# Moving the mask and the slot values of a graph kernel's setup from VectorE to GpSimd

## The reference

```
x = layernorm(x + L0(x))   # gated graph network: 4 steps of  a[dst] += W[type] @ h[src] + b[type];  h = GRU(a, h)
x = layernorm(x + L1(x))   # GIN, two convolutions: h + sum over edges, then a two-layer perceptron
x = layernorm(x + L2(x))   # GCN: symmetric normalization, relu, batch norm
x = layernorm(x + L3(x))   # SAGE: weighted mean of the neighbours
```

## Time and profile before

| | us |
|---|---|
| median of 3 runs | 9466.73 (9453.7 to 9488.25) |
| profiled execution, its own time | 9465.41 |
| its span, first to last instruction | 9463.6 |
| TensorE busy | 6959.9 (74%) |
| VectorE busy | 5864.7 (62%) |
| GpSimd busy | 4695.3 (50%) |
| ScalarE busy | 4484.3 (47%) |

### The profile page before, as it was taken

The page is one execution under the profiler, slowest core; times in us unless marked ns, Lnnn a source line. Parts: engine busy times, 40 slices in busy tenths (PEclk is TensorE's granted clock), DMA queues, the critical chain, the costliest instruction groups (busy, mean ns, idle before and its releaser), DMA issues.

```text
span 9463.6 us, 174694 instructions
## 1 busy us (share of the span) xinstructions
PE 6959.9 (74%) x57107; PEld 5494.3 (58%) x57108; DVE 5864.7 (62%) x15303; ACT 4484.3 (47%) x11415; POOL 4695.3 (50%) x4469
## 2 busy tenths in 40 slices
PE   4666666668877887887777777666688876648988
PEld 2333333347767776776666566545466655537887
DVE  7888888856666665665777433222245533347998
ACT  0000000036655655565888666555566655534443
POOL 0000000027756765665666566567666656655554
PEclk7887777779999998998999888787778878879999
DMA  3211111159999999999999999999999999959897
GB/s 86 66 46 46 51 46 46 46 169 269 265 257 264 272 263 260 267 267 256 253 258 252 260 274 278 261 277 274 271 267 264 270 254 269 272 151 230 224 224 192
DMA packets 1185494, 2014.92 MB, mean 213 GB/s; under 512 B 421508, under 2 KB 864807, under 8 KB 1181690
## 3 DMA queue, kind: packets, MB, share of 16 engines
q1 hardware_dynamic: 916698, 1097.24, 46.9%
q10 hardware_dynamic: 126656, 689.26, 20.0%
q0 software_dynamic: 141280, 217.70, 10.3%
HBM read 1232.72 MB, written 770.89 MB: 212 GB/s over the span
## 4 chain that ended last, share of the span: by engine, by line
DMA 32%; issue 24%; PE 17%; DVE 14%; ACT 8%; DVEq 4%; SPq 2%; POOL 0%; ACTq 0%; POOLq 0%
DMA bounce<-work 17%; DMA work<-bounce 14%; PE ps_pair L1024 5%; ACT work L1270 5%; PE ps_agg L1041 3%; DVE hs L1779 2%; PE ps_agg L1038 2%; DVE work L1788 2%; DVE agg_sb L1820 2%; ACT L1296 1%; DVEq L1795 1%; DVEq L1777 1%; PE ps_gate L1101 1%; DVE work L1802 1%; ACT gate L1296 1%
## 5 line engine op out<-in xcount | busy, mean ns | idle before, releaser
L846 POOL DMA_INDIRECT work<-node_rows,work x4410 | 4638.7, 1052 | 2686.9 <-issue 1464.8
L1270 ACT ACTIVATE work<-ps_pair 120x384 bf16<-120x384 f32 x7344 | 3364.2, 488 | 1671.5 <-PE ps_pair L1024 1047.0
L1024 PE MATMUL ps_pair<-rows_now,work 128*128 128x192 bf16 x14688 | 2614.2, 267 | 727.4 <-ACT work L1270 435.4
L1024 PEld LDWEIGHTS ps_pair<-rows_now,work 128*128 128x128 fp8e4 x14688 | 1288.4, 104 | 1201.9 <-issue 1056.5
L1041 PE MATMUL ps_agg<-work 120*128 120x192 bf16 x6272 | 967.2, 287 | 394.7 <-DMA work<-bounce 381.2
L1769 DVE TENSOR_TENSOR work<-iota_bf,dl_all 120x2048 bf16<-120x2048 bf16 x882 | 1075.2, 1219 | 30.4 <-DMA rows_now<-node_rows 16.6
L1038 PE MATMUL ps_agg<-work 120*128 120x192 bf16 (+1 forms) x6272 | 843.0, 259 | 223.4 <-DMA work<-bounce 209.2
L852 POOL MEMSET work<- 128x32 bf16 x2 | 0.2, 124 | 1955.8 <-SPq L677 1955.8
L1041 PEld LDWEIGHTS ps_agg<-work 120*128 120x128 bf16 x6272 | 660.1, 115 | 464.7 <-issue 359.6
L1058 PE MATMUL ps_agg<-work 128*128 128x192 bf16 (+1 forms) x7840 | 911.9, 247 | 0.7 <-issue 0.6
L1038 PEld LDWEIGHTS ps_agg<-work 120*128 120x128 bf16 x6272 | 579.5, 102 | 250.5 <-issue 165.0
(11 more groups left out here) (314 smaller groups left out, 10909.0 us busy)
## 6 DMA issues: line engine op xcount, KB each, us to landing
bounce<-work ACTq DMA_DIRECT2D x918, 727.5 KB
work<-bounce SPq DMA_DIRECT2D x882, 727.5 KB
work<-src_onehots SPq DMA_DIRECT2D x918, 256.0 KB
work<-node_rows,work POOLq DMA_INDIRECT x4410
work<-grid_vals SPq DMA_DIRECT2D x49, 960.0 KB, 5.0
node_rows<-stage SPq DMA_DIRECT2D x686, 48.0 KB
rows_now<-node_rows SPq DMA_DIRECT2D x42, 768.0 KB, 13.6
src_onehots<-work SPq DMA_DIRECT2D x17, 1536.0 KB, 8.4
```

The costliest lines, as they stand in the source:

```text
L846: pool.indirect_dma_start(out=ring[:, at.slot3() * LB + b, 0:3 * H], out_offset=None, in_=table_of(at.p), in_offset=bass.IndirectOffsetOnA ...
L1024: last = mm(bank[:, a * 3 * H:(a + 1) * 3 * H], oh[s.buf()][:, 2 * m + a, :], rows_now[:, s.chunk() * CHUNK + 2 * m + a, :], start=a == 0, ...
L1270: a_(raw[s.raw()][0:ROWS, m // 2, 2 * (m % 2):2 * (m % 2) + 2, 0:3 * H], ps_pair[m % 2][0:ROWS, 0:6 * H].rearrange("p (b f) -> p b f", b=2 ...
```

## The change

In the loop over pairs:

- The comparison of columns (L1592) moves ahead of the first rank product. The mask (L1595) goes to GpSimd (`slot_values`), between the new semaphores `same_made` and `ahead_made`. The reduction into `ahead` (L1597) moves behind the second rank product, and waits for the mask.
- The source one-hots are made in two parts, for the first tile of the pair between the two rank products, for the second tile where both were.
- The values of the slots (L1632) and of the rest (L1661) are made by GpSimd, two instructions each. The place one-hots have a buffer each (`grid_at`, `left_at`). TensorE waits for the lane one-hots (`lanes_made`) and for the values of the rest (`left_made`) by two semaphores. SyncE's wait for `left_made` now is a wait for GpSimd.
- GpSimd does this for the pairs in order, ahead of its wait for the end of the setup.

```diff
@@ GpSimd, new
+        def slot_values(q, par):
+
+            two = win[par]
+            pool.wait_ge(same_made, q + 1)
+            pool.sem_inc(pool_ran, 1)
+            g.tensor_tensor(same, same, earlier.to_broadcast([P, 2, WC, WC]), ALU.mult).then_inc(ahead_made, 1)
+            pool.wait_ge(grid_known, q + 1)
+            pool.sem_inc(pool_ran, 1)
+            for t in range(2):
+                last = g.tensor_tensor(grid_now[:, t, :, :, :],
+                                       grid_at[:, t, :, :].rearrange("p n (o u) -> p n o u", o=1)
+                                       .to_broadcast([P, WC, GV, SLOTS]),
+                                       two[t][:, :, DL:W2 + 1].rearrange("p n (v o) -> p n v o", o=1)
+                                       .to_broadcast([P, WC, GV, SLOTS]), ALU.mult)
+            last.then_inc(grid_made, 1)
+            pool.wait_ge(left_known, q + 1)
+            pool.sem_inc(pool_ran, 1)
+            for t in range(2):
+                last = g.tensor_tensor(left_now[:, t, :, :, :],
+                                       left_at[:, t, :, :].rearrange("p n (b o) -> p n b o", o=1)
+                                       .to_broadcast([P, WC, LB, LV]),
+                                       two[t][:, :, 0:LV].rearrange("p n (o v) -> p n o v", o=1)
+                                       .to_broadcast([P, WC, LB, LV]), ALU.mult)
+            last.then_inc(left_made, 1)
...
@@ TensorE, place_pair
                 last.then_inc(grid_placed[t], 1)
+            pe.wait_ge(lanes_made, q + 1)
             pe.wait_ge(left_made, q + 1)
             if not first:
@@ VectorE, rank_pair
+            v.tensor_tensor(same, key.rearrange("p t (n o) -> p t n o", o=1).to_broadcast([P, 2, WC, WC]),
+                            key.rearrange("p t (o n) -> p t o n", o=1).to_broadcast([P, 2, WC, WC]), ALU.is_equal
+                            ).then_inc(same_made, 1)
             rank_in_lower(0)
-            v.tensor_tensor(same, key.rearrange("p t (n o) -> p t n o", o=1).to_broadcast([P, 2, WC, WC]),
-                            key.rearrange("p t (o n) -> p t o n", o=1).to_broadcast([P, 2, WC, WC]), ALU.is_equal)
-            dve.drain()
-            v.tensor_tensor(same, same, earlier.to_broadcast([P, 2, WC, WC]), ALU.mult)
-            dve.drain()
-            v.tensor_reduce(out=ahead, in_=same, axis=AX.X, op=ALU.add)
+            if spare_work is not None:
+                spare_work(0)
             dve.wait_ge(rank_folded[0], q + 1)
             rank_in_lower(1)
+            dve.wait_ge(ahead_made, q + 1)
+            dve.sem_inc(dve_ran, 1)
+            v.tensor_reduce(out=ahead, in_=same, axis=AX.X, op=ALU.add)
             if spare_work is not None:
-                spare_work()
+                spare_work(1)
...
-            at_place(rank)
-            dve.drain()
-            for t in range(2):
-                last = v.tensor_tensor(grid_now[:, t, :, :, :],
-                                       places[:, t, :, :].rearrange("p n (o u) -> p n o u", o=1)
-                                       .to_broadcast([P, WC, GV, SLOTS]),
-                                       two[t][:, :, DL:W2 + 1].rearrange("p n (v o) -> p n v o", o=1)
-                                       .to_broadcast([P, WC, GV, SLOTS]), ALU.mult)
-            last.then_inc(grid_made, 1)
+            at_place(grid_at, rank).then_inc(grid_known, 1)
...
-            at_place(batch)
+            at_place(left_at, batch).then_inc(left_known, 1)
             dve.drain()
             for t in range(2):
-                one_hots(lane_hot[t], P, lane_i, t)
-                last = v.tensor_tensor(left_now[:, t, :, :, :],
-                                       places[:, t, :, :].rearrange("p n (b o) -> p n b o", o=1)
-                                       .to_broadcast([P, WC, LB, LV]),
-                                       two[t][:, :, 0:LV].rearrange("p n (o v) -> p n o v", o=1)
-                                       .to_broadcast([P, WC, LB, LV]), ALU.mult)
-            last.then_inc(left_made, 1)
+                last = one_hots(lane_hot[t], P, lane_i, t)
+            last.then_inc(lanes_made, 1)
...
@@ VectorE, src_hot
+        def src_hot(q, j, waits, tiles=(0, 1)):
+
+            if 0 in tiles:
+                dve.wait_ge(lo_back, q * 32 + 32)
+                if waits is not None:
+                    dve.wait_ge(src_hot_stored, waits)
+                dve.sem_inc(dve_ran, 1)
...
-            for t in range(2):
+            for t in tiles:
...
+            if 1 not in tiles:
+                return
...
@@ VectorE, windows
-                src_hot(q - 2, 2 * ((u + 1) % 3), waits)
+                src_hot(q - 2, 2 * ((u + 1) % 3), waits, (t,))
```

More of the change, by code:

```diff
@@ L173, in build @@
     spare_i, batch_i = [c.take(2 * WC, i32).rearrange("p (t n) -> p t n", t=2) for _ in range(2)]
-    places = c.take(2 * WC * SLOTS, fp32).rearrange("p (t n u) -> p t n u", t=2, u=SLOTS)
+    grid_at, left_at = [c.take(2 * WC * SLOTS, fp32).rearrange("p (t n u) -> p t n u", t=2, u=SLOTS) for _ in range(2)]
     grid_now = c.take(2 * WC * GM, bf16).rearrange("p (t n v u) -> p t n v u", t=2, n=WC, u=SLOTS)
@@ L320, in build @@
     rank_folded = [sem(f"rank_folded{i}") for i in range(2)]
+    same_made = sem("same_made")
+    ahead_made = sem("ahead_made")
+    grid_known = sem("grid_known")
+    left_known = sem("left_known")
+    lanes_made = sem("lanes_made")
     grid_made = sem("grid_made")
@@ L837, in _ @@
                                 ).then_inc(open_row_in, 16)
+        def slot_values(q, par):
[21 more added lines that the diff above has]
+            last.then_inc(left_made, 1)
+        slot_values(0, 0)
+        slot_values(1, 1)
+        with pool.Fori(1, WPAIRS // 2) as i:
+            for par in range(2):
+                slot_values(i * 2 + par, par)
+        slot_values(WPAIRS - 1, 0)
         pool.wait_ge(setup_done, 1)
@@ L1622, in rank_pair, with at_place @@
             v.tensor_tensor(spare_pos, left_sum, left, ALU.subtract)
-            def at_place(numbers):
-                v.tensor_tensor(places, numbers.rearrange("p t (n o) -> p t n o", o=1).to_broadcast([P, 2, WC, SLOTS]),
+            def at_place(to, numbers):
+                return v.tensor_tensor(to, numbers.rearrange("p t (n o) -> p t n o", o=1).to_broadcast([P, 2, WC, SLOTS]),
                                 place_row[:, :].rearrange("p (a b u) -> p a b u", a=1, b=1)
                                 .to_broadcast([P, 2, WC, SLOTS]), ALU.is_equal)
-            at_place(rank)
-            dve.drain()
-            for t in range(2):
-                last = v.tensor_tensor(grid_now[:, t, :, :, :],
-                                       places[:, t, :, :].rearrange("p n (o u) -> p n o u", o=1)
-                                       .to_broadcast([P, WC, GV, SLOTS]),
-                                       two[t][:, :, DL:W2 + 1].rearrange("p n (v o) -> p n v o", o=1)
-                                       .to_broadcast([P, WC, GV, SLOTS]), ALU.mult)
-            last.then_inc(grid_made, 1)
+            at_place(grid_at, rank).then_inc(grid_known, 1)
             dve.wait_ge(base_summed, q + 1)
@@ L1704, in windows, with spare_work @@
             q = i * 6 + u
-            def spare_work():
+            def spare_work(t):
                 waits = (i * 2 + (u // 3)) * 16 if u % 3 == 2 else None
```

## The result

The changed kernel takes 9555.72 us (median of 6 runs, 9531.83 to 9585.17) against 9470.93 (6 runs): a ratio of 1.0094, 95% interval 1.0074 to 1.0115. It is slower, by 85 us; the forecast was 9608 us, 137 over the same kernel before. The profiled execution has a span of 9548.6 us, 85.0 over the one before, and the chip reaches the end of the setup (SyncE's first load for the passes) at 2079.9 us instead of 2006.1. So 74 us are the setup's. The 11 others lie in the passes, which are the same in both. Between single executions the passes differ by that much.

A forecast was written before the change was run, and what follows sets the result against it. VectorE's own chain was taken to set each setup pair, with short hand-overs to TensorE. Terms 1.3 - 0.5 + 0.6 + 1.5 = +2.9 us a pair, 49 pairs: +142 us, median 9608, range 9430 to 9740.

The forecast's parts named there:

- the hold: A VectorE instruction with two SBUF inputs, or an f32 tensor-scalar, begun inside a GpSimd product waits for its end.
- the likeliest case: All terms of the setup loop as summed: +2.9 us a pair, 9560 to 9660 us, chance 0.52.
- rival B: Half a hold: rank product first, or GpSimd's last product slips on; +0.2 to +1.3 us a pair, 9475 to 9530, chance 0.18.
- Comparison ahead of the rank product: On VectorE, its 0.83 us fits into the 1.12 us wait for ScalarE and costs nothing.
- Mask, forecast +1.3: First rank product begins inside GpSimd's mask and waits for its end: +1.3 us a pair, bounds 0 to 1.5.
- rival C: TensorE's clock falls at the first fold after longer idle time: +2.6 us a pair more, 9735 us, chance 0.13.
- Source one-hots in halves: VectorE around the second rank product: gain only in pairs not waiting for the second fold; mean -0.5 us, bounds -1.6 and 0.
- Grid values: VectorE loses 1.34 us of products, but L1643 and L1645 or a later tensor-scalar wait for GpSimd: net +0.6 us a pair.
- Values of the rest: VectorE loses 1.45 us, but lane one-hots and what follows stand in line with GpSimd's 2.90 us: net +1.5 us a pair.
- The forecast's other value for the grid: If L1645's integer tensor-scalars are held as well, the grid term is +1.0 instead of +0.6, the time 9628 us.
- Rival A: bf16 inputs or small strided tiles escape the hold: net -1.9 us a pair, 9375 to 9405 us, chance 0.17.

The follow-up runs named there:

- order-only: The changed kernel with nothing on GpSimd (mask, grid values and values of the rest on VectorE), new order kept: 9476.74 us, ratio 1.0001 to the kernel before.
- fillers: Products of ones on TensorE in its idle times, into a bank nobody reads; added to the kernel before 9446.48 us, the changed 9499.06, the order-only 9391.26.

## Why the prediction was right, and where its size was off

The direction was right, and so were the mechanism and the place for the values: the hold is real, sits at L1675, L1677 and the lane one-hots, and turns work taken off VectorE into a loss. The size was not: the sum was +2.9 us a pair, and the loop shows +1.31. The time, 9555.72 us, lies in the wide range but just under the 9560 to 9660 of the likeliest case, because the mask went as rival B has it (the rank product first); +1.31 is the upper end of B's +0.2 to +1.3. By its terms:

*Comparison ahead of the rank product:* free, as said, where the class sums keep their 4.78 us (the wait for ScalarE is 0.28 us instead of 1.12 then); order-only comes out at 38.04 us.

*Mask, forecast +1.3:* this term failed. The hold of the first rank product by the mask happened in full in 2 of 49 pairs (4.95 and 4.85 us, both early), and by 0.4 us at most in six more. In those two the first fold took 4.67 and 4.78 us as well, which is rival C. In the others either VectorE was first, because the class sums were faster (4.4 to 4.7 us instead of 4.78) and ScalarE's copy came 0.1 to 0.3 us sooner, and the mask then held L1720 for 1.1 us within the slack ahead of the first fold; or the class sums took 5.8 to 5.9 us (16 of the 42 pairs) and the copy came after the mask. I had named the race and its 0.2 us, and put the term at one end. The mask alone shows that end, and rival C behind it: 40.40 us a pair. In the changed kernel the two columns ahead of the second rank product grew by 0.35 us; 0.18 of that is there with the mask on VectorE too (9.41 us), with class sums of 5.03 us instead of 4.85. The whole of the mask's move costs 0.17 us a pair (39.35 against 39.18).

*Source one-hots in halves, forecast -0.5:* -0.33. I took the second fold as it was, 3.09 us in a quarter of the pairs (11 of 42) and 5.6 in the others, and the gain from the fast ones; in the changed kernel none of the 42 is under 4.78 us. It is 4.78 in the 26 quick pairs, where the gain comes from, and 5.7 to 5.9 in the others.

*Grid values, forecast +0.6:* +0.52. *Values of the rest, forecast +1.5:* +0.82. GpSimd's rate was 2.07 to 2.14 ns an element (540 in 1.16 us, 648 in 1.34), my lower bound, not 2.3. From the start of the lane one-hots to the end of L1694 lie 4.95 us, and 2.63 are the two one-hots undisturbed: the two products of the rest added 2.3 us, not 2.95. The rate explains 0.2 to 0.3 us of that; the rest of it I put down to the start of each product, which runs beside the one-hot ahead of it, and this isn't tested. Issue time at the pair's start (0.17 idle in the earlier trace rows) is hidden as well. The forecast's other value for the grid, +1.0 with L1645 held, wasn't reached, although its form was held (L1677, 1.34 us instead of 0.37): both holds together are 1.83 us against 1.34 us of work taken off.

*TensorE's clock:* I had it as rival C, at one place, to one side. It was the largest unknown of the case, on both sides: it made one edit (the mask alone) twice as dear as the hold (2.36 us a pair against 1.1), and two others (the values, one at a time) nearly free. Rival A is refuted: bf16 inputs (the rank product of 4.85 us), int16 inputs (L1608) and tiles of 2 columns (L1675) are held too.

Open: why a longer pair gives the class sums back their pace in one kernel and takes it in another. In the kernels without fillers a first fold takes 3.09 us where TensorE was idle for 1.3 to 1.9 us ahead of it, and 4.6 to 4.8 where it was 2.1 to 2.6; at 2.0 both occur. Elsewhere idle time alone doesn't tell: ahead of the second fold it is 3.85 to 4.0 us, and the fold takes from 3.1 to 5.9 us; 2.7 us ahead of the class sums were followed by 4.4 us in one pair of the changed kernel and by 5.9 in another. What TensorE did in the pair before must come in, and no run here isolates it.

## What to carry to other kernels

Elementwise work given to GpSimd beside a busy VectorE isn't parallel where GpSimd reads SBUF and VectorE's instructions have two SBUF inputs: count it in line, at 2.1 ns an element against VectorE's 0.8 (the mask, 648 in 0.50 us) to 1.3 (the values of the rest, 630 in 0.81), and expect a loss. Where TensorE waits on VectorE in every round, look at its idle times before counting microseconds: a hold of 1.1 us, in 29 of 42 rounds, cost 2.4 us a round in the mean, and cheap fillers made an order worth 1.1 us a round that was worth nothing without them. Test parts together as well as singly, since none of the single costs here added up.

## What was not expected of the hardware

GpSimd's memsets run beside VectorE instructions with two SBUF inputs, its products don't (0.16 against 1.02 us for the same instruction). TensorE's pace: one idle microsecond more ahead of a fold (2.54 instead of 1.45) and its 16 products took 4.78 instead of 3.09 us, and fillers of 256 columns in that idle time undid it in all pairs. In the loop of the order-only kernel the granted clock rose from 0.79 to 0.92 by fillers alone, and the time fell by 0.8% (from 1.0001 to 0.9923 of the kernel before timed beside each); in the kernel before it rose to 0.90 and the time fell by 0.24%.
